# Loading the node features once, in the order of 32-row blocks, and the adjacency rows of the message sweep to match

## The reference

```python
h = jnp.maximum(_layernorm(x, axis=-1), 0.0)
msg = adj.T @ h
inv_deg = 1.0 / adj.sum(axis=0)            # infinite values become 0
x = x + msg * inv_deg[:, None]
h = jnp.maximum(_layernorm(x, axis=-1), 0.0)
x1 = swish((adj @ h) @ W + b)
x2 = swish((adj @ x1) @ W + b)
return x + x2
```

## Time and profile before

| | us |
|---|---|
| median of three runs | 655.73 (652.41, 655.73, 656.75) |
| profiled execution | 652.93 |
| its span | 651.1 |
| busy: PE / POOL / DVE / ACT | 627.9 / 561.6 / 504.2 / 298.8 |
| moved by transfers | 199.82 MB, mean 307 GB/s |
| chain that ended last | PE 73%, DMA 16% |

### The profile page before, as it was taken

How to read it: one execution, slowest core, us unless ns; L and a number is a source line. 1 busy time by engine, 2 the same in 40 slices (tenths; PEclk the granted TensorE clock), 3 DMA queues, 4 the chain that set the end, 5 groups by cost and what they waited for, 6 DMA issues and landing times.

```text
span 651.1 us, 6791 instructions
## 1 busy us (share of the span) xinstructions
PE 627.9 (96%) x2232; PEld 403.4 (62%) x2232; DVE 504.2 (77%) x518; ACT 298.8 (46%) x372; POOL 561.6 (86%) x283
## 2 busy tenths in 40 slices
PE   7899999999999989999999999999999999999896
PEld 5355666567565456566667667666666666666563
DVE  3988889878847879687778777777787977976882
ACT  1475433643432164645445445445444445443452
POOL 2399799499796569998999999999999999998794
PEclk9899999999998989999999999999999999999999
DMA  8999999999999999999999999909999999999971
GB/s 272 356 374 332 344 342 365 307 329 366 320 260 328 323 347 336 307 330 284 347 348 310 348 347 322 287 1 211 309 347 335 327 337 323 334 342 304 331 210 33
DMA packets 155827, 199.82 MB, mean 307 GB/s; under 512 B 5520, under 2 KB 138896, under 8 KB 155792
## 3 DMA queue, kind: packets, MB, share of 16 engines
q1 hardware_dynamic: 91568, 136.07, 66.8%
q10 hardware_dynamic: 64224, 63.32, 32.9%
HBM read 197.26 MB, written 2.10 MB: 306 GB/s over the span
## 4 chain that ended last, share of the span: by engine, by line
PE 73%; DMA 16%; POOL 3%; DVE 3%; issue 2%; SPq 2%; ACT 1%; DVEq 0%; POOLq 0%; ACTq 0%
PE dg L393 20%; DMA raw<-in_adj_dram 16%; PE m_ps L316 14%; PE dg L410 9%; PE dg L399 9%; PE dg L400 9%; PE m_ps L336 3%; PE m_ps L321 3%; PE m_ps L322 3%; DVE turned L660 2%; POOL at_lo L778 2%; PE m_ps L419 2%; PE tp L364 1%; POOL a_lo L764 1%; SPq L230 1%
## 5 line engine op out<-in xcount | busy, mean ns | idle before, releaser
L778 POOL TENSOR_TENSOR at_lo<-turned,at_hi 128x1024 fp32r<-128x1024 f32 x160 | 379.5, 2408 | 20.5 <-ACT at_hi L511 11.4
L660 DVE STREAM_TRANSPOSE turned<-raw 128x1024 f32<-128x1024 f32 x256 | 302.3, 1222 | 79.5 <-PE dg L393 46.8
L511 ACT ACTIVATE at_hi<-turned 128x1024 fp32r<-128x1024 f32 x160 | 169.3, 1061 | 201.3 <-DVE turned L660 152.8
L393 PE MATMUL dg<-turned,f_w 128*128 128x512 f32 x384 | 182.1, 597 | 2.2 <-issue 2.2
L764 POOL TENSOR_TENSOR a_lo<-raw,a_hi 128x1024 fp32r<-128x1024 f32 x62 | 145.9, 2388 | 32.3 <-ACT a_hi L480 32.3
L616 DVE TENSOR_TENSOR dg<-raw,dg 128x2048 f32<-128x2048 f32 x60 | 137.6, 2293 | 38.0 <-DMA raw<-in_adj_dram 35.8
L399 PE MATMUL dg<-at_hi,f_hi 128*128 128x512 f32 x320 | 133.9, 418 | 2.0 <-ACT at_hi L511 2.0
L410 PE MATMUL dg<-at_lo,f_hi 128*128 128x512 f32 x320 | 130.2, 488 | 1.0 <-POOL at_lo L778 1.0
L400 PE MATMUL dg<-at_hi,f_lo 128*128 128x512 f32 x320 | 126.4, 395 | 0.0
L316 PE MATMUL m_ps<-raw,h 128*128 128x512 f32 x264 | 120.1, 601 | 6.3 <-DMA raw<-in_adj_dram 6.3
L393 PEld LDWEIGHTS dg<-turned,f_w 128*128 128x128 f32 x384 | 72.7, 190 | 57.7 <-issue 49.5
(11 more groups left out here) (50 smaller groups left out, 251.2 us busy)
## 6 DMA issues: line engine op xcount, KB each, us to landing
raw<-in_adj_dram SPq DMA_DIRECT2D x64, 1024.0 KB, 7.8
raw<-in_adj_dram SPq DMA_DIRECT2D x120, 512.0 KB, 11.4
raw<-in_adj_dram ACTq DMA_DIRECT2D x120, 512.0 KB, 12.4
x<-in_x_dram SPq DMA_DIRECT2D x16, 128.0 KB, 8.1
out_dram<-zs SPq DMA_DIRECT2D x12, 128.0 KB, 14.5
h<-in_x_dram SPq DMA_DIRECT2D x1, 768.0 KB, 9.5
h<-in_x_dram SPq DMA_DIRECT2D x1, 256.0 KB, 3.3
out_dram<-zs SPq DMA_DIRECT2D x4, 64.0 KB, 1.8
```

Source lines behind the costliest of these rows:

```text
L393: mm = pe.matmul(acc, f_w[:, UC * WHOLE3.index(j) + c], turned[:, unit % TURN, c], start=first and c == 0, stop=False)
L511: act.activation(at_hi[:, s % RING3], turned[:, unit % TURN], ACT.Copy).then_inc(hi3_done, 1)
L660: dve.transpose(dst, src).then_inc(t3_done, 1)
L778: pool.tensor_tensor(at_lo[:, s % RING3], turned[:, unit % TURN], at_hi[:, s % RING3].bitcast(f32), ALU.subtract).then_inc(lo3_done, 1)
```

## The change

- The features are loaded once, in the head, into `x` and in the order of the blocks of 32 (`load_nodes`, each call four transfers to 32 partitions). The 16 later transfers and their semaphores are gone, and so are the three transfers to `h`.
- VectorE's statistics and ScalarE's normalisation read `x`; ScalarE writes `h` as before.
- Since `h` now has the order of the blocks, the adjacency rows of sweep 1 are loaded in that order too: a pair is four transfers, one for each block of 32 partitions, 256 KB each, all from SP's queue. The users of `raw1` wait for 64 in place of 16.
- In the head, pairs 1 and 2 now stand ahead of the second half of the features.

```diff
--- before.py
+++ after.py
@@ -21,7 +21,6 @@
 WHOLE1_FIRST = (0, 1, 2, 3, 4, 5, 7, 10, 13, 15)
 LATE_ROWS = (2, 3, 5)
 SPLIT_ROWS = (6, 8, 9, 11, 12, 14) + LATE_ROWS
-NODES_AT = (3, 6, 9, 12)
 
 
 SB = 32
@@ -54,8 +53,8 @@
     f32, f32r = mybir.dt.float32, mybir.dt.float32r
     ALU, ACT = mybir.AluOpType, mybir.ActivationFunctionType
 
-    x_tiles = x_in.rearrange("(t p) d -> p t d", p=P)
-    adj_tiles = adj.rearrange("(t p) c -> p t c", p=P)
+
+    adj_rows = adj.rearrange("(q b m c) n -> q b c m n", b=P // SB, m=QT, c=SB)
     adj_blocks = adj.rearrange("(t p) c -> p t c", p=SB)
     nodes = "(q b m c) d -> q b c m d"
     x_nodes = x_in.rearrange(nodes, q=QUARTERS, b=P // SB, m=QT, c=SB)
@@ -118,7 +117,6 @@
         tp = ps("tp", [P, 2, 512])
 
         x_loaded = [sem(f"x_loaded{b}") for b in range(len(HEAD))]
-        nodes_loaded = [sem(f"nodes_loaded{q}") for q in range(QUARTERS)]
         w_loaded, b_loaded = sem("w_loaded"), sem("b_loaded")
         consts_set, consts_ready = sem("consts_set"), sem("consts_ready")
         raw1_loaded = [sem(f"raw1_loaded{n}") for n in range(RAW1)]
@@ -266,20 +264,29 @@
                         sp.wait_ge(main1_done, back + 1)
                     else:
                         sp.wait_ge(lo1_done, 2 * split1(back) + 2)
-                sp.dma_start(raw1[:, v % RAW1], adj_tiles[:, 2 * k:2 * k + 2, q * QC:(q + 1) * QC])\
-                  .then_inc(raw1_loaded[v % RAW1], 16)
-
-            for b, (lo, hi) in enumerate(HEAD):
-                sp.dma_start(h[:, lo:hi], x_tiles[:, lo:hi]).then_inc(x_loaded[b], 16)
-                load1(b)
-            for v in range(len(HEAD), QUARTERS * PAIRS):
+                rows, m = 2 * k // QT, 2 * k % QT
+                for b in range(P // SB):
+                    sp.dma_start(raw1[b * SB:(b + 1) * SB, v % RAW1],
+                                 adj_rows[rows, b][:, m:m + 2, q * QC:(q + 1) * QC])\
+                      .then_inc(raw1_loaded[v % RAW1], 16)
+
+            def load_nodes(n, q, m0, m1):
+                for b in range(P // SB):
+                    sp.dma_start(x[b * SB:(b + 1) * SB, q * QT + m0:q * QT + m1], x_nodes[q, b][:, m0:m1])\
+                      .then_inc(x_loaded[n], 16)
+
+            load_nodes(0, 0, 0, QT // 2)
+            load1(0)
+            load_nodes(1, 0, QT // 2, QT)
+            load_nodes(1, 1, 0, QT)
+            load1(1)
+            load1(2)
+            load_nodes(2, 2, 0, QT)
+            load_nodes(2, 3, 0, QT)
+            for v in range(3, QUARTERS * PAIRS):
                 load1(v)
                 if v in PIECE0_SP:
                     load3(sp, 0, SP_BLOCKS[PIECE0_SP.index(v):][:1])
-                if v % PAIRS in NODES_AT:
-                    q, b = v // PAIRS, NODES_AT.index(v % PAIRS)
-                    sp.dma_start(x[b * SB:(b + 1) * SB, q * QT:(q + 1) * QT], x_nodes[q, b])\
-                      .then_inc(nodes_loaded[q], 16)
             for i in range(1, len(PIECES)):
                 if i not in KEPT:
                     load3(sp, i, SP_BLOCKS)
@@ -302,7 +309,7 @@
                 cols = slice(half * 512, (half + 1) * 512)
                 acc = m_ps[:, cols]
                 if half == 0:
-                    pe.wait_ge(raw1_loaded[v % RAW1], 16 * (v // RAW1 + 1))
+                    pe.wait_ge(raw1_loaded[v % RAW1], 64 * (v // RAW1 + 1))
                     if whole1(v):
                         pe.wait_ge(h_ready, 2 * k + 2)
                     else:
@@ -461,8 +468,8 @@
                         act.wait_ge(norm_ready, b + 1)
                 for t in (2 * k, 2 * k + 1):
                     if k in splits1:
-                        relu(h_hi[:, 2 * SPLIT_ROWS.index(k) + t % 2], h[:, t], t)
-                    relu(h[:, t], h[:, t], t).then_inc(h_ready, 1)
+                        relu(h_hi[:, 2 * SPLIT_ROWS.index(k) + t % 2], x[:, t], t)
+                    relu(h[:, t], x[:, t], t).then_inc(h_ready, 1)
 
             def round_late(k):
 
@@ -471,7 +478,7 @@
                 act.activation(h_hi[:, r:r + 2], h[:, 2 * k:2 * k + 2], ACT.Copy).then_inc(late_rounded, 1)
 
             def hi1(v):
-                act.wait_ge(raw1_loaded[v % RAW1], 16 * (v // RAW1 + 1))
+                act.wait_ge(raw1_loaded[v % RAW1], 64 * (v // RAW1 + 1))
                 for i in range(2):
                     s = 2 * split1(v) + i
                     if s >= RING1:
@@ -601,12 +608,12 @@
                 return ins
 
             def head(b):
-                dve.wait_ge(x_loaded[b], 16)
-                statistics(h, range(*HEAD[b]), b).then_inc(mv_ready, 1)
+                dve.wait_ge(x_loaded[b], 64 if b == 0 else 128)
+                statistics(x, range(*HEAD[b]), b).then_inc(mv_ready, 1)
 
             def add_degrees(v):
                 src = raw1[:, v % RAW1]
-                dve.wait_ge(raw1_loaded[v % RAW1], 16 * (v // RAW1 + 1))
+                dve.wait_ge(raw1_loaded[v % RAW1], 64 * (v // RAW1 + 1))
                 if v % PAIRS == 0:
                     if v > 0:
                         dve.wait_ge(degs_ready, v // PAIRS)
@@ -634,8 +641,6 @@
             def add_message(q, part):
                 dve.wait_ge(msg_turned, 3 * q + 2 + part)
                 dve.wait_ge(inv_ready, q + 1)
-                if part == 0:
-                    dve.wait_ge(nodes_loaded[q], 16 * (P // SB))
                 for m in range(QT // 2):
                     k = part * (QT // 2) + m
                     row = x[:, q * QT + k, :]
```

## The result

The changed kernel takes **738.41 us** (median of four runs, 726.05 to 742.66). The kernel before took 654.38 us in the same session. The medians lie 84 us apart. The ratio is 1.118, with a 95% interval of 1.102 to 1.134: it is taken from the two faster runs alone (726.05 and 736.89), since the other two count as executions in a slower state, and by it the loss is 77 us. The forecast was 714 us, in a range of 653 to 750.

The account below looks back on a forecast made before the run. Message sweep bound by TensorE in its middle and transfers at its end; 1.2 us + 71.3 MB at 250 GB/s + 4.9 us starts the second sweep at 291.3 us, 58.5 later, giving 714 us, range 653 to 750.

Parts of the forecast that it names:

- the rival without overlap: Message sweep: the two partition halves never overlap, rate 224 GB/s, second sweep at 324.4 us, 747 us in all; chance 0.25.
- What bounds and what comes after: Message sweep bound by TensorE in the middle, transfers at the end; the later sweeps only shift as one block.
- The mechanism: Adjacency loads of the message sweep: partitions 0 to 63 reach only half the 16 ports; one queue nearly alone gives 224 GB/s.
- The bytes: Message sweep: features loaded once remove 2.1 MB of 73.4, leaving 71.3 MB to carry.
- The rate, "I take 250 GB/s": Adjacency loads on one queue in the message sweep: 250 GB/s taken, with ends of 224 and 347.
- Issue at 0: SP in the message sweep: four issues add 1.5 us a pair, costed at nothing because SP's waiting for buffers covers them.
- Head at 0: Head: adjacency pairs 1 and 2 ahead of the last 1 MB of features cost 0, ends -2 and +4 us.
- The x transfers, at most 7.7 us: Transfer-bound stretches of the message sweep: dropping the later feature loads, about 1.1 us each, gains at most 7.7 us.
- Clock at 0: TensorE in the message sweep: stalls may lower its clock, but waiting for transfers covers slow stretches, so 0.
- "SP waits little for buffers": Message sweep: a sign that the forecast is right, against 77.6 + 75.7 us of SP's buffer waits before.
- The rival that the rate stays over 315 GB/s: Message sweep: engines spread over both halves, TensorE still bounds the middle, about 652 us; chance 0.19.
- its second form: Message sweep: rate stays over 315 GB/s and every transfer wait goes, up to 9.8 us gained, 648 us; chance 0.07.

## Why the prediction was right, and which term was mis-sized

The 738.41 us lie in the stated range of 653 to 750, which says little: it holds nearly no change and a loss of 14% alike. They lie outside the forecast's own case (235 to 285 GB/s, 679 to 735 us) and in that of the rival without overlap (735 to 750 us, chance 0.25). The direction, the cause and the sum were right; one term of the sum was mis-sized, the rate.

- **What bounds and what comes after** held: the windows over 175 to 216 us and the chain named the transfers as the next bound, and the 418 us behind the sweep stayed 417.9.
- **The mechanism** held: one queue of 32-partition transfers has the rate of one half alone. The earlier trace rows gave 224 to 233 GB/s, the changed kernel ran at 223 to 232 in slices 2 to 12, and the two kernels with 64 partitions alone showed that the half is the cause. The prediction had said that the earlier trace rows differ only in the halves; they differ in the number of queues too, and only these runs separated the two.
- **The bytes** held: 71.3 MB in 317.06 - 6.1 = 311 us is 229 GB/s in the mean, which is what the slices show.
- **The rate, "I take 250 GB/s"**, is the term that was off, by 21 GB/s or 25.8 us: 291.3 us were forecast for the second sweep and 317.06 came. The case of no overlap, 324.4 us and 747, was nearer in both. The 250 leaned on the 258 GB/s of a 2 us window in which most of the bytes went to 128 partitions. Such a mixture is no price for a queue without one such transfer. The rows with one queue nearly alone were of the kind that was asked for. The spreading of the engines that was to lift the rate exists only late and little: 227 GB/s up to slice 11, then up to 264.
- **Issue at 0** held within 2.3 us (0.35% of 652.5), which is all that four transfers to 128 partitions with smaller packets cost.
- **Head at 0** held for the order of the loads (1.0016). That the head's features now go to 32 partitions was not run by itself.
- **The x transfers, at most 7.7 us**, measured 6.2 (3.9 to 8.5). The prediction said that this gain exists only if the adjacency keeps its rate; it didn't.
- **Clock at 0** held as a cost. It fell in windows of the sweep, to 0.85 in one, and TensorE's busy time grew from 627.9 to 663.2 us, but the transfers' share of 1.03 to 1.05 says that this lay under their time.
- **"SP waits little for buffers"** was wrong: 151 us, as before. A queue-bound sweep holds its buffers in flight, so the issuer waits for one all the same.
- **The rival that the rate stays over 315 GB/s** had 0.26 with its second form. Behind its first slice the changed kernel's queue gave 223 to 264, and even two queues gave 304 at best over 4 us and 227 to 271 in the first sixteen slices.

## What to carry to other kernels

Before a transfer to all 128 partitions is cut into parts, ask which half each part fills. In these runs a queue that fills 0 to 63 and 64 to 127 by separate transfers carried about 225 GB/s, and transfers that span both went at over 400, even with 64 partitions, as long as all the engines carried them and none to a single half stood in the same queue. Four transfers in place of one cost 0.35%. Then read rate and engine share together: here a low rate at full share was a half being written, and a low rate at a quarter share was a transfer on few engines. And before a load is merged away at the price of an order, try moving it to a stretch where another engine bounds.

## What the runs showed that was not expected

- A transfer whose source's slowest dimension is 4 ran at 105 GB/s with 26% of the engines, and SP's issue of it took 4.8 us in the median in place of 0.43.
- In the changed kernel the rate climbs by itself from 226 to 264 GB/s through a uniform sweep; in the order 0, 2, 1, 3 it reaches 250 by the eighth slice and stays near it (244 to 254) to the sixteenth. That engines drift apart is a guess.
- A queue that mixes transfers across the middle with transfers to 32 partitions ran at 240 GB/s, where the sum of the two kinds gives 295.
